# Attention beside a state-space scan: two score banks, a later maximum, parked gates and gelu inputs

## What is computed

```python
# mamba, for each of 256 channels and 16 states
h_t = exp(d_t * A) * h_(t-1) + d_t * B_t * x_t
y_t = sum_n(h_t * C_t) + x_t * D
h   = x + (y * silu(z)) @ out_proj.T
# attention on h, after an rms norm
attn = softmax(where(causal, -inf, q @ k.T * scale))
x    = h + (attn @ v) @ o_w.T
# gated feed-forward, after an rms norm
x1 = x + (silu(xn @ gate.T) * (xn @ up.T)) @ down.T
# ternary feed-forward: Wq has values -1, 0, 1
x2 = x1 + layernorm(gelu(layernorm(x1) @ Wq_fc.T)) @ Wq_proj.T
```

## Time and profile before

| | |
|---|---|
| median of three runs | 1120.97 us (1120.17 to 1122.46) |
| the profiled execution, by its own time | 1119.09 us |
| its span, first to last instruction | 1117.3 us |
| mean granted clock of TensorE | 0.735 of full |
| HBM read and written | 82.7 and 4.8 MB |

### The profile page before, as it was taken

One profiled execution on the slowest core, in us unless ns is written; L12 is line 12 of the kernel. 1 busy time (PEld: TensorE's weight loads), 2 busy tenths in 40 slices (PEclk: granted clock), 3 DMA queues, 4 the chain that ended last, 5 costly groups with the idle time before them and its releaser, 6 DMA issues. The chain is left out here.

```text
span 1117.3 us, 9176 instructions
## 1 busy us (share of the span) xinstructions
PE 780.9 (70%) x3056; PEld 486.8 (44%) x3056; DVE 577.3 (52%) x580; ACT 485.9 (43%) x899; POOL 387.2 (35%) x209
## 2 busy tenths in 40 slices
PE   5576775667857757787857787757786675550997
PEld 1244443445424435444525444525443444440665
DVE  1497963446523415633425533425866979940443
ACT  2666424224443335543335534335566464310443
POOL 0265532224412203421203421203544556605223
PEclk9787766657867656887556878656896896565999
DMA  5634300530005300000800000800025034333000
GB/s 140 248 132 159 145 1 0 191 122 1 19 0 184 110 20 1 1 1 4 309 0 1 1 0 4 309 0 1 1 85 219 1 117 187 133 93 96 16 23 22
DMA packets 34280, 86.44 MB, mean 77 GB/s; under 512 B 6947, under 2 KB 13466, under 8 KB 34202
## 3 DMA queue, kind: packets, MB, share of 16 engines
q1 hardware_dynamic: 32954, 83.20, 21.3%
q0 software_dynamic: 1280, 2.66, 0.7%
HBM read 82.66 MB, written 4.80 MB: 78 GB/s over the span
## 5 line engine op out<-in xcount | busy, mean ns | idle before, releaser
L423 POOL TENSOR_TENSOR hc<-hst,bc 128x1024 f32<-128x1024 f32 x128 | 302.0, 2360 | 593.2 <-DVE hst L890 520.1
L551 ACT ACTIVATE dA<-delta,m_A_s 128x511 f32<-128x511 f32 x256 | 176.1, 715 | 371.7 <-DVE hst L890 365.7
L890 DVE TENSOR_TENSOR_SCAN hst<-dA,bank 128x1024 f32<-128x1024 f32 x128 | 292.1, 2282 | 2.6
L1202 PE MATMUL bank<-ident,hc 128*128 128x128 f32 x1024 | 180.7, 336 | 38.5 <-POOL hc L423 38.5
L925 DVE TENSOR_REDUCE nmax<-bank 128x1 f32<-128x384 f32 (+3 forms) x44 | 28.3, 643 | 321.3 <-PE bank L1125 321.3
L1202 PEld LDWEIGHTS bank<-ident,hc 128*128 128x128 f32 x1024 | 156.4, 178 | 70.9 <-POOL hc L423 48.2
L881 DVE TENSOR_TENSOR bank<-bank,bc 128x1024 f32<-128x1024 f32 x128 | 157.2, 1228 | 13.6 <-ACT bank L540 5.0
L1125 PE MATMUL bank<-arena 128*128 128x32 f32 (+5 forms) x576 | 142.6, 395 | 7.5 <-ACT arena L619 3.0
L1125 PEld LDWEIGHTS bank<-arena 128*128 128x128 f32 (+1 forms) x576 | 94.8, 241 | 35.2 <-issue 23.7
L1289 PE MATMUL bank<-ident,arena 128*128 128x128 f32 x160 | 36.5, 365 | 63.9 <-ACT arena L629 28.3
L1289 PEld LDWEIGHTS bank<-ident,arena 128*128 128x128 f32 x160 | 25.5, 189 | 81.9 <-issue 50.1
(11 more groups left out here) (205 smaller groups left out, 943.3 us busy)
## 6 DMA issues: line engine op xcount, KB each, us to landing
bc<-crows SPq DMA_DIRECT2D x128, 512.0 KB, 8.8
bc<-in_w SPq DMA_DIRECT2D x1, 4096.0 KB, 12.8
xin<-in_xT SPq DMA_DIRECT2D x8, 256.0 KB, 5.1
sorted_rows<-in_blank SPq DMA_DIRECT2D x1, 1584.0 KB, 7.6
arena<-sorted_rows SPq DMA_DIRECT2D x1, 1320.0 KB, 7.0
conv<-in_m_cw SPq DMA_DIRECT2D x2, 512.0 KB, 3.6
crows<-prow SPq DMA_DIRECT2D x8, 64.0 KB, 1.6
out_rows<-zs,target POOLq DMA_INDIRECT x24, 2.2
```

What stands on the lines that cost most here:

```text
L423: pool.tensor_tensor(hc[:, g % HCRING], hst[:, g % HRING], bc[:, p, 1], ALU.mult) \
L551: act.activation(dA[:, g % RING, j, 1:], delta[:, h, 1:], ACT.Exp, scale=M[mamba_of(c)]["A"][:, h, n:n + 1]).then_inc(sems["dA"], 1)
L890: dve.tensor_tensor_scan(hst[:, g % HRING].rearrange(flat), dA[:, g % RING].rearrange(flat), bank[:, DB:DB + 2, :].rearrange(flat), 0.0, A ...
L1202: last = pe.matmul(bank[:, YB, P * j:P * j + P], hc[:, g % HCRING, n, P * j:P * j + P], ident[:], start=False, stop=s % PAIRS == PAIRS - 1 ...
```

## The change

- Scores alternate between banks 7 and 6 (`score_bank`), and each fill is transposed within its own bank. Fill n has its scores at slot `A_START[n]`, maximum and exp two half-steps later, transposes and copy three, the product with v four later. `probT` has two slots instead of four.
- The products with v have v as the stationary operand (32 columns) and write the output already turned, 32 partitions a head, into bank 2 (`PVB`). All four query tiles gather there. Their normalisation is one step at the end: a reciprocal of 512 values (each sum 32 times), four transposes of it through bank 6, a copy, and one product. The turn of the attention output and its copy go.
- As bank 2 is taken, the steps in `SINGLE` (25 to 84) do product and scan in two halves of 512 in bank 1.
- `RING` is 4. The semaphores of the broadcast rows count two pairs of states each.
- z, the gates and the fc products (scaled) are parked by copies as they come (`z_park`, `gate_park`, `fcp`), and silu and gelu run later from SBUF: z as one of 1024 columns, gates as 1024 and 512, the gelu four times 512.
- The gelu output is scaled on GpSimd (four `tensor_scalar`), and turned by plain transposes; the diagonals go.
- The tables `TAIL`, `HEAD`, `FAT`, `A0`, `F0` change; `AAT` holds attention's other slots.

The diff, cut:

```diff
-DU, DB, YB, HB, FB5, SB6, TB7 = 0, 1, 3, 4, 5, 6, 7
-RING = 3
+DU, DB, PVB, YB, HB, FB5, SB6, TB7 = 0, 1, 2, 3, 4, 5, 6, 7
+RING = 4
-TAIL = dict(ycp1=3, back1=5, gate1=6, out=7, res=8, ycp0=20, back0=31, gate0=32)
-HEAD = (dict(raw0=10, park0=11, raw1=13, park1=15, z0=17, visit=20, z1=20, xp=23, prow=24, dt0=25, sp0=26, delta0=27,
-             du0=28, decay=28, dt1=33, sp1=34, delta1=35, du1=36),
-        dict(cen=14, cp=15, var=16, rs=17, xn=18, raw0=19, park0=21, raw1=22, park1=23, z0=24, visit=25, z1=25, xp=27,
-             prow=28, dt0=29, sp0=30, delta0=30, du0=31, decay=31, dt1=33, sp1=34, delta1=35, du1=36))
-A0 = 9
-F0 = 14
-FAT = dict(sq=1, var=2, rs=3, nrm=4, gate=6, visit=7, up=9, gu=10, down=13, x1=14, cen=15, cp=16, st=17, rst=18, fc=19,
-           gelu=20, hsq=22, hr=23, dg=24, turn=25, tc=26, proj=31, x2=32)
+TAIL = dict(ycp1=3, back1=4, gate1=5, out=6, res=7, ycp0=19, back0=31, gate0=32)
+HEAD = (dict(raw0=10, park0=11, raw1=12, park1=13, z0=14, zp0=15, z1=16, zp1=17, visit=18, xp=20, prow=21, dt0=22, sp0=23,
+             delta0=25, du0=26, decay=27, dt1=33, sp1=33, delta1=35, du1=36),
+        dict(cen=12, cp=13, var=14, rs=15, xn=16, raw0=18, park0=19, raw1=20, park1=21, z0=22, zp0=22, z1=23, zp1=23,
+             visit=24, xp=26, prow=26, dt0=27, sp0=27, delta0=29, du0=30, decay=30, dt1=33, sp1=33, delta1=35, du1=36))
+A0 = 8
+F0 = 9
+AAT = dict(sq=0, var=1, rs=1, nrm=2, qk=4, qkc=4, v=5, vc=5, rec=29, rb=30, rbc=30, norm=31, o=32, h1=33)
+A_START = (6, 8, 10, 12, 14, 16, 18, 20, 22, 24, 26)
+A_LAG = dict(max=2, exp=2, turn=3, copy=3, pv=4)
+FAT = dict(sq=1, var=2, rs=2, nrm=3, gate=5, park=5, xh=6, visit=8, up=8, gu=9, down=14, x1=15, cen=16, cp=16, st=17,
+           rst=17, fc=18, fcp=18, gelu=22, hsq=23, hr=23, scale=24, turn=26, tc=26, proj=30, x2=31)
 NAT = dict(cen=0, sq=1, var=2, rs=3, xl=4, sq2=5, rms=6, rs2=7, xn=8)
 NSTART = {1: 0, 2: 10, 3: 20}
-
-
-def turn_slot(n):
-    return 10 + 2 * n + (1 if n - 1 in LAST_FILL else 0)
+SINGLE = range(25, 85)
...
+            def z_park(c, h):
                 act.wait_ge(sems["z"], 2 * c + h + 1)
                 if c >= 2:
                     act.wait_ge(sems["out"], c - 1)
-                act.activation(zs[:, c % 2, h], bank[:, HB, :], ACT.Silu).then_inc(sems["zs"], 1)
+                act.activation(zs[:, c % 2, h], bank[:, HB, :], ACT.Copy).then_inc(sems["zp"], 1)
 
             def silus(c, i):
-                if c is not None:
-                    silu_z(c, 0)
-                if i is not None:
-                    gate_silu(i, 0)
                 if c is not None:
                     act.wait_ge(sems["park"], 2 * c + 2)
                     act.activation(xs_pair(c), xs_pair(c), ACT.Silu).then_inc(sems["xs"], 1)
+                    act.wait_ge(sems["zp"], 2 * c + 2)
+                    act.activation(zs[:, c % 2], zs[:, c % 2], ACT.Silu).then_inc(sems["zs"], 1)
                 if i is not None:
-                    gate_silu(i, 1)
-                if c is not None:
-                    silu_z(c, 1)
-                if i is not None:
-                    gate_silu(i, 2)
+                    act.wait_ge(sems["f_park"], FB * (i + 1))
+                    act.activation(gs[:, 0:2], gs[:, 0:2], ACT.Silu).then_inc(sems["f_gs"], 1)
+                    rows = FFN_ROWS[2]
+                    act.activation(gs[0:rows, 2], gs[0:rows, 2], ACT.Silu).then_inc(sems["f_gs"], 1)
                 act.preload_act_table_set(EXP_LN)
 
             def project_rows(c):
...
+                    width = keys * len(heads)
+                    if a == A_START[n] + A_LAG["exp"]:
                         act.wait_ge(sems["a_max"], done)
                         if done >= 3:
                             act.wait_ge(sems["a_t"], done - 2)
+                        if n == 0 and i >= 1:
+                            act.wait_ge(sems["a_rec"], i)
                         for at, hd in enumerate(heads):
                             act.activation(prob[:, n % 2, keys * at:keys * at + keys],
-                                           bank[:, SB6, keys * at:keys * at + keys], ACT.Exp,
+                                           bank[:, score_bank(n), keys * at:keys * at + keys], ACT.Exp,
                                            bias=nmax[:, N_HEADS * j + hd:N_HEADS * j + hd + 1],
                                            accum_out=psums[:, j, hd:hd + 1]).then_inc(sems["a_exp"], 1)
-                    if a == turn_slot(n) + 1:
+                    if a == A_START[n] + A_LAG["copy"]:
                         act.wait_ge(sems["a_t"], done)
-                        if n - 1 in LAST_FILL or n == 0:
-                            if QB * i + j >= 1:
-                                act.wait_ge(sems["a_pv"], QB * i + j)
-                        width = keys * len(heads)
-                        at = (heads[0] * keys) // T if j != 2 else heads[0]
-                        act.activation(probT[:, at, 0:width], bank[:, TB7, 0:width], ACT.Copy).then_inc(sems["a_tc"], 1)
-                if a == 35:
-                    act.wait_ge(sems["a_oT"], i + 1)
-                    act.activation(qs, bank[:, TB7, :], ACT.Copy).then_inc(sems["a_oc"], 1)
+                        if done >= 3:
+                            act.wait_ge(sems["a_pv"], done - 2)
+                        act.activation(probT[:, n % 2, 0:width], bank[:, score_bank(n), 0:width], ACT.Copy) \
+                            .then_inc(sems["a_tc"], 1)
+                if a == AAT["rbc"]:
+                    act.wait_ge(sems["a_rb"], i + 1)
...
+                    if f == FAT["fcp"] + j:
+                        act.wait_ge(sems["f_rst"], i + 1)
                         act.wait_ge(sems["f_fc"], QB * i + j + 1)
                         if j < FB:
                             act.wait_ge(sems["f_gu"], FB * i + j + 1)
-                        act.activation(gs[:, j], bank[:, FB5, :], ACT.Gelu, scale=rs1[:, j:j + 1],
-                                       accum_out=hsum[:, j:j + 1]).then_inc(sems["f_gelu"], 1)
+                        act.activation(gs[:, j], bank[:, FB5, :], ACT.Copy, scale=rs1[:, j:j + 1]) \
+                            .then_inc(sems["f_fcp"], 1)
+                if f == FAT["gelu"]:
+                    act.wait_ge(sems["f_fcp"], QB * (i + 1))
+                    for j in range(QB):
+                        act.activation(gs[:, j], gs[:, j], ACT.Gelu, accum_out=hsum[:, j:j + 1]).then_inc(sems["f_gelu"], 1)
                     act.preload_act_table_set(EXP_LN)
...
+                if g in SINGLE:
+                    dve.tensor_tensor(bank[:, DB, :], bank[:, DU, :], bc[:, p, 0, 0], ALU.mult).then_inc(sems["half"], 1)
+                else:
+                    if g == SINGLE[-1] + 1:
+                        dve.wait_ge(sems["a_norm"], SEQS)
+                    dve.tensor_tensor(bank[:, DB:DB + 2, :], bank[:, DU:DU + 1, :].to_broadcast([P, 2, T]), bc[:, p, 0],
+                                      ALU.mult).then_inc(sems["dbu"], 1)
             def scan(g):
+                p = g % PAIRS
                 flat = "p j t -> p (j t)"
+                if g in SINGLE:
+                    dve.wait_ge(sems["half"], halves_before(g) + 1)
+                    dve.wait_ge(sems["dA"], 2 * g + 1)
+                    if g >= HRING:
+                        dve.wait_ge(sems["hc"], g - HRING + 1)
+                    dve.tensor_tensor_scan(hst[:, g % HRING, 0], dA[:, g % RING, 0], bank[:, DB, :], 0.0, ALU.mult, ALU.add) \
+                        .then_inc(sems["half"], 1)
+                    dve.wait_ge(sems["half"], halves_before(g) + 2)
+                    dve.tensor_tensor(bank[:, DB, :], bank[:, DU, :], bc[:, p, 0, 1], ALU.mult).then_inc(sems["dbu"], 1)
+                    dve.wait_ge(sems["dbu"], g + 1)
+                    dve.wait_ge(sems["dA"], 2 * g + 2)
+                    dve.tensor_tensor_scan(hst[:, g % HRING, 1], dA[:, g % RING, 1], bank[:, DB, :], 0.0, ALU.mult, ALU.add) \
+                        .then_inc(sems["scan"], 1)
+                    return
...
+                    if a == A_START[n] + A_LAG["pv"]:
+                        pe.wait_ge(sems["a_tc"], done)
+                        if n == 0:
+                            pe.wait_ge(sems["a_vc"], i + 1)
+                            if i == 0:
+                                pe.wait_ge(sems["scan"], SINGLE[0])
+                            else:
+                                pe.wait_ge(sems["a_norm"], i)
+                        for t in range(j + 1):
+                            for at, hd in enumerate(heads):
+                                last = mm(bank[HD * hd:HD * hd + HD, PVB, P * j:P * j + P], vs[:, t, HD * hd:HD * hd + HD],
+                                          probT[:, n % 2, keys * at + P * t:keys * at + P * t + P], t == 0, t == j)
+                        last.then_inc(sems["a_pv"], 1)
+                    if a == A_START[n] + A_LAG["turn"]:
                         pe.wait_ge(sems["a_exp"], exps)
```

(13 more changed lines are left out.)

190 lines of the change are left out of this document (84 added, 106 removed).

## The result

The changed kernel takes 897.88 us (median of 896.42 to 900.35) against 1120.57, a ratio of 0.801 (95%: 0.799 to 0.804): 223 us less, where 116 were forecast. The sign was right. The profiled execution took 900.35 us with a span of 898.6, and the mean granted clock rose from 0.735 to 0.834. In the table of the experiments e1 and e7 hold slow runs, more than 1.5% above the fastest of the same kernel: two of e1's four (911.9 and 917.1, against 898.3 and 900.8) and one of e7's (931.4, against 917.5 to 919.9).

What follows compares the result with a forecast made beforehand. The prediction held that hand-overs bound the kernel, no engine being full. Savings in blocks 1 to 6, -116 us together, took the profiled 1119.1 to 1003, and the median's 1.9 offset gave 1005 us, range 930 to 1075.

Steps and rivals of the forecast that it cites:

- coupling: Full blocks: 12 us added for engines coupled in fixed order, a guess scaled up from block 0.
- low clock: Full blocks: 10 us added for stretches where TensorE runs at the lower level of its clock.
- a sum of 119: Full block of 16 steps: the busiest engine's work in each step, TensorE at its high level, added up to 119 us.
- the opening of the loop: Attention steps: two banks, later maximum and exp, and ring of four end a 7.9 us round trip; a 4.5 us chain remains.
- the line of the slots: Moved slots: earlier normalised input removes a 5.1 us wait, y's copy comes earlier; joint semaphore costs at most 2 us a block.
- Rival (b): ScalarE replaces the loop: copy and exp wait behind silus, gelus and squares, half the gain stays; 1065 us, chance 20%.
- Rival (a): Looser than thought: engines overlap across steps, coupling and low level nearly vanish, full blocks near 119; 945 us, chance 25%.
- Rival (c): TensorE's clock stays at its low level, a full block taking 182 us; 1172 us in all, chance 5%.
- Halved steps: Steps 25 to 84: product and scan in halves cost VectorE 0.3 us a step, 18 us (0 to 30).
- Products with v: Attention: 80 instructions of 128 columns, 10.5 against 9.3 us a sequence; taken as nothing, bounds -3 and +3.
- The reciprocal: VectorE, step 2 of a block: 512 values at once take 4.6 us, delaying scan and next maximum by up to 4.6.
- Rival (d): Scores stay a step late, the loop stays closed and VectorE's extra 32 us lie on the path; 1153 us, chance 3%.

Runs made afterwards that it cites:

- e1: The changed kernel with each maximum in the same half-step as its scores (lag 0 instead of 2): 906.4 us, ratio 0.809.
- e7: The changed kernel with one score bank, transposes ahead of the next scores, maximum lag 0, exp lag 1, decay ring of three: 919.5 us, ratio 0.818.
- e13: The kernel before with only A0 = 8 instead of 9, attention one half-step earlier: 1011.7 us, ratio 0.902.
- e3: The changed kernel with the decay ring back at three instead of four: 895.6 us, ratio 0.799.
- e16: The changed kernel with only A0 = 9 instead of 8, attention one half-step later: 871.9 us, ratio 0.776.
- e18: e16 (the changed kernel with A0 = 9) with a decay ring of three: 870.5 us, ratio 0.775.
- e14: e7 (the changed kernel with its loop undone) with A0 = 9 instead of 8: 1038.8 us, ratio 0.925.
- e15: e14 with a decay ring of four instead of three: 945.5 us, ratio 0.843.
- e17: e16 (the changed kernel with A0 = 9) with each maximum in the half-step of its scores: 934.7 us, ratio 0.833.
- e11: The changed kernel with product and scan in halves for 43 more steps, from 25 to the end: 909.8 us, ratio 0.810.
- e10: The changed kernel with attention wholly as before, A0 = 8, F0 = 12, no halved steps, ring of three; parking and new HEAD and TAIL stay: 996.6 us.
- e12: The changed kernel with the reciprocal of the 16 sums, then a copy spreading it to 512 values: 898.2 us, ratio 0.802.
- e4: The changed kernel with silu and gelu reading straight from the bank again, without parking: 924.0 us, ratio 0.825.
- e9: e7 with silu and gelu straight from the bank and the old slot tables; new products with v, halves and GpSimd scaling stay: 1142.8 us.

## Why the prediction was right in sign and too small in size

In the prediction's own terms two steps failed. One is the size: coupling (12 us) and low clock (10 us), added in each full block to a sum of 119, were worth nothing there, and the sum itself was too high for blocks 1, 2 and 5. The other is the cause: the opening of the loop was put down to banks, lag and ring, where the place of attention does as much, and the line of the slots left it out.

**The diagnosis.** Right: hand-overs bound the kernel, the loop of the earlier trace rows was there, and once opened the time of a step is set by the work of an engine. The signs that were named came: maxima 20 us (below 60), decays 33 (below 100), all the waits before the fc products together 7.6 us (none above 5), clock in the full blocks 0.86 and 0.87 (above 0.8). Rival (b) fell: exps and copies cost TensorE some 10 us a full block, not over 25.

**What opened the loop: wrong as told, and the step overlooked.** The prediction gave the opening to banks, lag and ring. All three together are worth 22 us where the change puts attention (e7); half of the gain comes with A0 = 8 in the old kernel (e13). "The slots" had a few lines in the prediction, on the normalised input, y's copy and the broadcast, and A0 was not in them. What the runs show in its place: the half-step of attention (parity), ring and lag each go far to open the same loop. Where enough of the others stand, one can be taken out for little or nothing (e1, e3, e16, e18); where they don't, parity is worth 109 (e13) and 119 (e7 to e14), the ring 93 (e14 to e15), the lag 63 (e16 to e17). So the mechanism was right for the place A0 = 9 and idle at the place that the change uses. A closer look at the earlier trace rows would have told it: the order product, maximum, scan, and the exp behind the decays, are the two facts that the half-step turns round.

**The size.** For a full block the sum of the largest engine in each step was 119; measured are 117 and 116. Added to it were 12 for coupling, a guess, and 10 for the clock, and these 22 us were the error, as 141 stood against 117 and 116. Blocks 2, 1 and 5, with smaller additions, were forecast 25, 19 and 10 us too long (127, 106 and 102 against 102, 87 and 92), block 6 two too short (73 against 75). These six blocks make up 101 of the 103 us by which the span was forecast too long. The coupling term had been scaled up from block 0 (69 us for a sum of 60), which itself went to 62: what block 0 showed was delay that the change removed. And where steps have slack, not even the sum of the per-step maxima is a floor: block 1 came out at 87 for a sum of 98, and e16 has 99 and 101 for 119, since one engine's long step lies beside another's short one. That the bare 119 came within 3 us is partly luck. From scan start to scan start block 3 has steps of 13.5, 11.6 and 12.2 us, where no step of the working is over 9.9. Its third, fourth and thirteenth take 5.1, 5.0 and 4.3 us, where the working has 9.9, 8.9 and 8.5 (such a step can lie half a step off one of the working). High and low cancel. Rival (a), "looser than I think", was the right direction at 945, with 25%. It had the full blocks right, near 119, and gave the four others 16 us more, where they came out 52 us shorter than forecast.

**The clock.** By the same working TensorE did spend 13 us more in a full block than at the high level (99 against 86), near the 10 that were added, but the block did not last longer than the sum for it. The granted clock was 0.86 and 0.87 with TensorE idle for 17 us of a block, 0.92 and 0.96 with 9 and 10 us (e16), and 0.72 with 43 us. Idle time alone doesn't set it: in e7's block 3 it is 0.97 with 21 us idle.

```profile
321.00:433.70 112.70, 91.97 (x439) 51.48 (x438) 77.31 (x88) 76.14 (x149) 51.28 (x27) 0.97 0.22 79
```

Rival (c) fell. In the last mamba block the clock is 0.62 again with 24 us of idle. The Trainium skill, "TensorE: Matmul & The Clock Gate", section "Part 4: PE-mode transpose", holds that transposes don't count as busy for the gate in the way that other products do. That block fits, as it did before. But in the full blocks the clock rose although the change had put sixteen transposes a sequence in place of products, and no run here separates transposes from idleness.

**The prices.** Halved steps: right (e11). Products with v: 41.6 us for the 320, 10.4 a sequence against 10.5 forecast; whether the fills with several heads side by side ran shorter is told by no run, and what their new place in the step is worth is open (e10). The reciprocal: 3.35 us, not 4.6; the line through 4 and 16 values was carried too far, 6.3 ns for each value beyond the fourth and not 8.75; and it was on no path (e12), where up to 4.6 us had been charged. GpSimd's scaling is 1.55 us, not 1.27, so 6.2 a sequence, inside the bounds of 3 and 8:

```profile
L391 POOL TENSOR_SCALAR arena<-arena,hvar 128x512 f32<-128x512 f32 x16 | 24.8, 1564 | 31.8 <-ACT hvar L695 31.8
L1406 PE MATMUL bank<-ident,arena 128*128 128x128 f32 x64 | 12.9, 338 | 9.1 <-POOL arena L391 9.1
```

It is waited for once, 9.1 us, in block 6, where no attention covers it. The start was charged nothing and cost 8 us: 4.5 of them since the parked z stands ahead of the silu of x (e4), the rest open. Steps with only attention were to take 4.5 to 6 us; in block 1 they take 4.3 to 6.0, but for one of 9.4.

**Rival (d)** was priced at 1153 for a loop that stays closed with VectorE's new work on it. e9 comes near that case, 1143: the loop is closed and VectorE has the new work, with the old slots as the condition. That the 22 us above the kernel before are VectorE's is not shown, as e9 differs from it in more.
